# An LSTM step with its four gates multiplied in four parts instead of three, in another order

## What is computed

```
combined = jnp.concatenate((x_t, h_prev), axis=1)
f_t = sigmoid(combined @ W_f + b_f)
i_t = sigmoid(combined @ W_i + b_i)
c_tilde = tanh(combined @ W_c + b_c)
c_t = f_t * c_prev + i_t * c_tilde
o_t = sigmoid(combined @ W_o + b_o)
h_t = o_t * tanh(c_t)
```

## Time and profile before

| | us |
|---|---|
| median of 3 runs | 2969.48 |
| lowest and highest run | 2964.39, 2971.04 |
| the profiled execution | 2961.34 |
| its span, first to last instruction | 2959.6 |

### The profile page before, as it was taken

How to read it: one execution, slowest core, us unless ns; L and a number is a source line. 1 busy time by engine, 2 the same in 40 slices (tenths; PEclk the granted TensorE clock), 3 DMA queues, 4 the chain that set the end, 5 groups by cost and what they waited for, 6 DMA issues and landing times. The chain is left out here.

```text
span 2959.6 us, 117784 instructions
## 1 busy us (share of the span) xinstructions
PE 2674.2 (90%) x44608; PEld 2439.2 (82%) x44608; DVE 2071.1 (70%) x6141; ACT 1901.5 (64%) x5006; POOL 1612.1 (54%) x2677
## 2 busy tenths in 40 slices
PE   7999999978888888868888889999999999999957
PEld 5777777777777777758888888999999999999956
DVE  6887888744444444457777777777777788888868
ACT  4666666644444444447777777787787678888824
POOL 6777777600000000046666665666666678888844
PEclk9999999999999999979999999999999999999979
DMA  3111111000000000020000001100000000000002
GB/s 97 36 36 36 36 37 43 13 11 13 12 13 13 12 13 13 12 81 22 23 21 25 21 21 36 51 9 9 9 9 9 28 31 9 9 9 9 8 22 92
DMA packets 110837, 74.60 MB, mean 25 GB/s; under 512 B 51504, under 2 KB 109360, under 8 KB 110512
## 3 DMA queue, kind: packets, MB, share of 16 engines
q1 hardware_dynamic: 96800, 61.03, 7.1%
q10 hardware_dynamic: 13968, 12.72, 1.5%
HBM read 51.68 MB, written 22.02 MB: 25 GB/s over the span
## 5 line engine op out<-in xcount | busy, mean ns | idle before, releaser
L1613 PE MATMUL g_H<-g_hT_upper,g_w_upper 128*128 128x256 f32 x1536 | 465.9, 303 | 5.6 <-DVE g_hT_rest L1357 5.5
L1641 PE MATMUL g_F<-g_w_upper,g_act_upper 128*128 128x256 f32 x1408 | 406.4, 289 | 60.2 <-DVE g_act_rest L1390 60.2
L1613 PE MATMUL g_H<-g_hT_rest,g_w_upper 128*128 128x256 f32 x1536 | 437.1, 285 | 0.0
L1613 PE MATMUL g_H<-g_hT_upper,g_w_rest 128*128 128x256 f32 x1536 | 437.0, 284 | 0.0
L1189 ACT ACTIVATE g_act_raw<-g_H,g_small 128x256 f32<-128x256 f32 x768 | 319.0, 470 | 143.2 <-PE g_H L1613 142.0
L1641 PE MATMUL g_F<-g_w_upper,g_act_rest 128*128 128x256 f32 x1408 | 396.3, 281 | 0.0
L1641 PE MATMUL g_F<-g_w_rest,g_act_upper 128*128 128x256 f32 x1408 | 396.3, 281 | 0.0
L762 POOL COPY l_xt<-seq 128x64 f32 x256 | 60.5, 236 | 599.0 <-PE l_O L773 595.3
L1641 PEld LDWEIGHTS g_F<-g_w_upper,g_act_upper 128*128 128x128 f32 x1408 | 265.9, 189 | 71.5 <-DVE g_act_rest L1390 71.2
L330 ACT ACTIVATE a_probs<-a_S,a_nmax 128x256 f32<-128x256 f32 x512 | 236.3, 479 | 118.4 <-DVE a_nmax L424 85.3
L1613 PEld LDWEIGHTS g_H<-g_hT_upper,g_w_upper 128*128 128x128 f32 x1536 | 297.0, 193 | 13.4 <-issue 9.3
(11 more groups left out here) (224 smaller groups left out, 8410.7 us busy)
## 6 DMA issues: line engine op xcount, KB each, us to landing
gmask<-masks ACTq DMA_DIRECT2D x97, 128.0 KB, 2.0
x<-in_x_dram SPq DMA_DIRECT2D x32, 256.0 KB, 3.0
a_adj<-in_adj_dram SPq DMA_DIRECT2D x32, 256.0 KB, 2.7
hidden<-l_hs SPq DMA_DIRECT2D x512, 16.0 KB, 1.4
seq<-hidden SPq DMA_DIRECT2D x32, 256.0 KB, 2.7
out_dram<-q_res SPq DMA_DIRECT2D x32, 256.0 KB, 2.1
masks<-gmask SPq DMA_DIRECT2D x32, 128.0 KB, 1.7
g_w_raw<-in_L_gnn_W_dram SPq DMA_DIRECT2D x6, 512.0 KB, 3.9
```

What stands on the lines that cost most here:

```text
L1613: last = pe.matmul(hidden_bank[m // 2][:, m % 2 * N:(m % 2 + 1) * N], w[:, c, m * P:(m + 1) * P], x[:, c, :], start=(c == 0 and k == 0), s ...
L1641: last = pe.matmul(ff_bank[:, it * D:(it + 1) * D], x[:, m, it * P:(it + 1) * P], w[:, m, :], start=(m == 0 and it == 0 and k == 0), stop= ...
```

## The change

The part with candidate and input is split. There are four banks of 64 columns each, in two copies, and the parts go in the order forget, candidate, input, output, for the bias, for x and for the hidden state. ScalarE takes the tanhs in that order, one more than before; only forget, input and output announce their end to others, since ScalarE's candidate tanh comes before its input tanh. VectorE forms `kept` first, when the forget gate is there, then `fresh` when the input gate is, then the cell. `ic` becomes the two tiles `ti` and `tc`. The number of VectorE operations and waits is unchanged.

```diff
--- before.py
+++ after.py
@@ -724,17 +724,17 @@
         xt = [sb(f"xt{i}", [P, KC, B]) for i in range(2)]
         hT = sb("hT", [P, KC, B])
         cell = sb("cell", [P, HQ])
-        ic, f, to, og = sb("ic", [P, 2, HQ]), sb("f", [P, HQ]), sb("to", [P, HQ]), sb("og", [P, HQ])
+        ti, tc, f, to, og = (sb(n, [P, HQ]) for n in ("ti", "tc", "f", "to", "og"))
         kept, fresh, tanh_c = sb("kept", [P, HQ]), sb("fresh", [P, HQ]), sb("tanh_c", [P, HQ])
         hs = [sb(f"hs{i}", [P, SEG, HQ]) for i in range(2)]
 
-        ic_bank, f_bank, o_bank = ([ctx.enter_context(nc.psum_tensor(f"l_{n}{i}", [P, 512], F32)) for i in range(2)]
-                                   for n in "GFO")
+        f_bank, c_bank, i_bank, o_bank = ([ctx.enter_context(nc.psum_tensor(f"l_{n}{i}", [P, 512], F32)) for i in range(2)]
+                                          for n in "FCIO")
 
         xt_done, xt_free, hT_done = sem("xt_done"), sem("xt_free"), sem("hT_done")
-        ic_ps, f_ps, o_ps = sem("ic_ps"), sem("f_ps"), sem("o_ps")
-        ic_done, f_done, to_done, og_done, tanh_done = (sem(n) for n in ("ic_done", "f_done", "to_done", "og_done", "tanh_done"))
-        kept_done, cell_done, h_done = sem("kept_done"), sem("cell_done"), sem("h_done")
+        f_ps, c_ps, i_ps, o_ps = sem("f_ps"), sem("c_ps"), sem("i_ps"), sem("o_ps")
+        i_done, f_done, to_done, og_done, tanh_done = (sem(n) for n in ("i_done", "f_done", "to_done", "og_done", "tanh_done"))
+        fresh_done, cell_done, h_done = sem("fresh_done"), sem("cell_done"), sem("h_done")
         stored = [sem("stored0"), sem("stored1")]
         STEPS = 2 * SEG
 
@@ -764,29 +764,29 @@
             @block.tensor
             def _(pe):
                 def step(n, u):
-                    parts = ((ic_bank[u % 2], slice(0, 2), ic_ps), (f_bank[u % 2], slice(2, 3), f_ps),
-                             (o_bank[u % 2], slice(3, 4), o_ps))
-
-                    def multiply(bank, gates, x, w, stop):
+                    parts = ((f_bank[u % 2], 2, f_ps), (c_bank[u % 2], 1, c_ps), (i_bank[u % 2], 0, i_ps),
+                             (o_bank[u % 2], 3, o_ps))
+
+                    def multiply(bank, gate, x, w, stop):
                         for c in range(KC):
                             for j in range(Q):
-                                last = pe.matmul(bank[j * B:(j + 1) * B, 0:(gates.stop - gates.start) * HQ], x[:, c, :],
-                                                 w[:, c, gates, j * HQ:(j + 1) * HQ], start=False,
+                                last = pe.matmul(bank[j * B:(j + 1) * B, 0:HQ], x[:, c, :],
+                                                 w[:, c, gate, j * HQ:(j + 1) * HQ], start=False,
                                                  stop=(stop and c == KC - 1), skip_group_check=True, tile_position=(0, j * B))
                         return last
 
-                    for bank, gates, _ in parts:
+                    for bank, gate, _ in parts:
                         for j in range(Q):
-                            pe.matmul(bank[j * B:(j + 1) * B, 0:(gates.stop - gates.start) * HQ],
-                                      t.pick[:, j * B:(j + 1) * B], t.bias_parts[:, gates, :],
+                            pe.matmul(bank[j * B:(j + 1) * B, 0:HQ],
+                                      t.pick[:, j * B:(j + 1) * B], t.bias_parts[:, gate, :],
                                       start=True, stop=False, skip_group_check=True, tile_position=(0, j * B))
                     pe.wait_ge(xt_done, n + 1)
-                    for bank, gates, _ in parts:
-                        last = multiply(bank, gates, xt[u % 2], wx, False)
+                    for bank, gate, _ in parts:
+                        last = multiply(bank, gate, xt[u % 2], wx, False)
                     last.then_inc(xt_free, 1)
                     pe.wait_ge(hT_done, n + 1)
-                    for bank, gates, done in parts:
-                        multiply(bank, gates, hT, wh, True).then_inc(done, 1)
+                    for bank, gate, done in parts:
+                        multiply(bank, gate, hT, wh, True).then_inc(done, 1)
 
 
                 pe.sem_inc(xt_free, 2)
@@ -797,10 +797,12 @@
             @block.scalar
             def _(act):
                 def step(n, u):
-                    act.wait_ge(ic_ps, n + 1)
-                    act.activation(ic[:, :, :], ic_bank[u % 2][:, 0:2 * HQ], ACT.Tanh).then_inc(ic_done, 1)
                     act.wait_ge(f_ps, n + 1)
                     act.activation(f[:, :], f_bank[u % 2][:, 0:HQ], ACT.Tanh).then_inc(f_done, 1)
+                    act.wait_ge(c_ps, n + 1)
+                    act.activation(tc[:, :], c_bank[u % 2][:, 0:HQ], ACT.Tanh)
+                    act.wait_ge(i_ps, n + 1)
+                    act.activation(ti[:, :], i_bank[u % 2][:, 0:HQ], ACT.Tanh).then_inc(i_done, 1)
                     act.wait_ge(o_ps, n + 1)
                     act.activation(to[:, :], o_bank[u % 2][:, 0:HQ], ACT.Tanh).then_inc(to_done, 1)
                     act.wait_ge(to_done, n + 1)
@@ -816,14 +818,14 @@
             def _(dve):
                 def step(s, u):
                     n, half = s * STEPS + u, u // SEG
-                    dve.wait_ge(ic_done, n + 1)
-                    dve.scalar_tensor_tensor(out=fresh[:, :], in0=ic[:, 0, :], scalar=1.0, in1=ic[:, 1, :],
-                                             op0=ALU.add, op1=ALU.mult)
                     dve.wait_ge(f_done, n + 1)
                     dve.wait_ge(cell_done, n + 1)
                     dve.scalar_tensor_tensor(out=kept[:, :], in0=f[:, :], scalar=1.0, in1=cell[:, :],
-                                             op0=ALU.add, op1=ALU.mult).then_inc(kept_done, 1)
-                    dve.wait_ge(kept_done, n + 1)
+                                             op0=ALU.add, op1=ALU.mult)
+                    dve.wait_ge(i_done, n + 1)
+                    dve.scalar_tensor_tensor(out=fresh[:, :], in0=ti[:, :], scalar=1.0, in1=tc[:, :],
+                                             op0=ALU.add, op1=ALU.mult).then_inc(fresh_done, 1)
+                    dve.wait_ge(fresh_done, n + 1)
                     dve.scalar_tensor_tensor(out=cell[:, :], in0=kept[:, :], scalar=0.5, in1=fresh[:, :],
                                              op0=ALU.mult, op1=ALU.add).then_inc(cell_done, 1)
                     dve.wait_ge(tanh_done, n + 1)
```

## The result

The changed kernel is slower by 0.18%: a ratio of 1.0018 to the kernel before, with a 95% interval of 1.0012 to 1.0024, from 20 runs of each. The medians are 2970.07 us (2963.0 to 2977.05) and 2964.12 us. So the difference by the ratio is some 5.3 us, 3.6 to 7.1. Forecast were +3.3 us and, on a base of 2969.48, a time of 2972.8.

What follows compares the result with a forecast made beforehand. No engine is full: the LSTM step, 2.581 us, is a loop of waits from the matmuls through tanhs, cell and transpose. A step 0.013 us longer, 256 times, adds 3.3 us to 2969.48, giving 2972.8; range 2961.5 to 2986.

Steps and rivals of the forecast that it cites:

- The chain keeps its shape: LSTM step: intervals behind the deciding part stay; input part ends at 0.880 us against forget's old 0.867, 0.013 later.
- The start price of 25 ns: TensorE's first group from idle: 25 ns extra, now on the forget part (0.432 us), later parts spaced by 0.224.
- Two narrow parts cost what a wide one does: TensorE's spacing in the LSTM step: two 64-column parts take 0.448 us against 0.435 for one of 128.
- ScalarE has room: ScalarE in the LSTM step: tanhs stay 0.224 us apart and the added activation costs nothing on the path.
- Kept and the loop's turn are covered: VectorE's kept hides in the wait for the input gate; 0.38 us of slack covers TensorE's work at the turn.
- The sum: 256 steps, each 0.013 us longer, add 3.3 us to the base of 2969.48: 2972.8 us, +0.11%.
- The instruction store: Rival: TensorE's four-step body of 1152 loads and matmuls isn't held; 90 to 180 us, some 3060 to 3150; chance 0.03.
- The held start: Rival: forget's second group waits after idle, up to 0.066 us a step, +17 us, 2986; chance 0.12 for over 0.2%.

Runs made afterwards that it cites:

- The order alone: Kernel before with forget first, candidate and input together second and uncut, and kept formed before fresh: ratio 1.0050, steady period 2.6346 us.
- the split alone: Changed kernel put back in the old order (candidate, input, forget, output, 64 columns each; kept formed after fresh): ratio 1.0021, steady period 2.5915 us.

## Why the prediction was right

The step of the chain was understood and its price nearly so; the forecast time, 2972.8 against 2970.07, is closer than the account deserves. Its base, the median of three runs, was 5.4 us above the median of twenty (2964.12), and its change, 3.3 us, 2.7 below the difference of the medians (5.95); the two errors have opposite signs. By its steps:

- *The chain keeps its shape, and only the end of the third narrow part against the second part counts.* Right. The order alone shows it with a sum of its own by the same rule (0.057 forecast, 0.054 found), the change itself with 0.013 forecast and 0.011 found, and the split alone has the changed kernel's period whichever gate is third.
- *The start price of 25 ns in the first group, then the usual spacing.* Right: the long pass is 244 ns, the forget part 0.431 (0.432 forecast), input's tanh at 0.95 (0.94).
- *Two narrow parts cost what a wide one does.* Right, within the 0.011: candidate, input and output start 0.22 to 0.23 apart.
- *ScalarE has room.* Right, and by more than thought: a tanh holds it for 0.11 to 0.12 us.
- *Kept and the loop's turn are covered.* Right: VectorE idles 0.22 between kept and fresh, and twice as many turns of TensorE's loop leave the period as it was.
- *The sum.* 3.3 us forecast; 2.8 are found in the step. The measured 5.3 has a second term, 2 to 3 us, that the prediction put at nothing: the first turn. So the mechanism accounts for about half of the loss, and the rest of the agreement in size is luck.
- *The instruction store.* The rival asked only whether 1152 loads and matmuls are held, and they are. That bringing them in the first time takes longer than using them, it passed over. It could have been read: the first turn of the kernel before shows stops of 0.36 and 0.67 us on issue, and a third more instructions a step had to lengthen them. Its price for a body that isn't held (90 to 180 us) was too low by far: it reckoned one wait a turn, but every block is waited for, which cost some 500 us at 2304. The case itself, 1152 not held, didn't arise.
- *The held start* didn't happen: forget's 0.43 excludes it.
- *The range.* Its lower end, 2964.39 less 3.1, is 2961.3 and not 2961.5; nothing hangs on it.

Whether the measured 5.3 us is "no change" by the bound of 0.2% or just beyond it the interval (1.0012 to 1.0024) leaves open; that it is slower than before is clear.

## What to carry to other kernels

Where a recurrent step is a loop of waits, write down the end of the part that the chain waits for last, in the old order and in the new, and add what follows it; taking one operation off the chain gains nothing when another of the same length takes its place. Cutting a part in two adds instructions even where it adds no time in a steady step: count the loop body in code blocks, since its first pass runs at the pace at which they arrive, and beyond some length (between 1728 and 2304 loads and matmuls here) every pass does. A wait whose value has to be computed belongs where its engine idles, not in front of the operation that the chain waits for: here moving one gave as much (5.3 us) as the change cost.

## What the runs showed of the hardware that I had not expected

- Instructions reached TensorE in blocks of 256 at one per 3.6 to 4.1 us in a loop's first pass, while the changed kernel's steady step uses 256 in 2.3 us. A body of 1728 loads and matmuls stayed in the store, one of 2304 was brought in anew in each turn, at 1.17 times the whole kernel's time. The Trainium skill (Runtime: NRT & Kernel Launch, "Instruction fetch mechanics") gives TensorE room for 2048 instructions, and the two bodies lie on either side of that. It also says that fetching is hidden because dispatch is slower than the fill; the stops of 1.3 to 2.4 us contradict that for matmuls as narrow as these.
- A tanh of 128x64 shows 0.22 us but lets the next one start after 0.11 to 0.12 us.
- Stops for instructions can cost the clock too: with TensorE busy for 0.45 us of the 2 us from 618 to 620, the granted clock was 0.60 in the next 2 us and 0.55 in the 2 after, and a step took 3.25 us instead of 2.57.
- A wait ahead of VectorE's product, for a value that depends on the loop's turn, cost 0.09 us in one step of four, and none when moved to the step's start.
